# Setup products of a graph attention layer moved into the layer before, norm sums moved to GpSimd, and one group of small products over four PSUM banks

## What is computed

```python
# layer 2, H = 4 heads
Wh = einsum('bni,hoi->bhno', h, W) + bW
e = einsum('bhno,hop->bhnp', Wh, attn)
scores = einsum('bhnp,bhmp->bhnm', e, Wh)
A_mat = tanh(where(adj, scores, 0))
hp = relu(einsum('bhnm,bhmo->bhno', A_mat, Wh))
ha = concat_heads(hp) @ A_w.T;  hf = h @ fc_w.T
coeff = sigmoid(hf @ g1_w.T + ha @ g2_w.T + gbias)
out = hf * coeff + ha * (1 - coeff)
# layer 3, 8 heads of 32, m = embs @ map_w.T + map_b
n = m / maximum(norm(m per head), 1e-8)
cos_adj = (n @ n.T masked) > 0.1
q = m @ q_w.T + q_b;  k = m @ k_w.T + k_b
p_attn = softmax(masked q @ k.T / sqrt(32)) * keep
adj = cos_adj * p_attn
sem = embs @ gcn_map_w.T + gcn_map_b
out = relu((adj @ sem @ gcn_W.T) / (adj.sum(-1) + 1))
```

## Time and profile before

| | before |
|---|---|
| median of 3 runs | 1966.75 us (1961.3 to 1969.16) |
| profiled execution, own time | 1959.6 us |
| its span | 1957.8 us |
| its mean granted TensorE clock | 0.985 |
| busy: TensorE | 1865.9 us (95%) |
| busy: VectorE, ScalarE, GpSimd | 1315.1, 865.8, 613.5 us |

### The profile page before, as it was taken

The page is one execution under the profiler, slowest core; times in us unless marked ns, Lnnn a source line. Parts: engine busy times, 40 slices in busy tenths (PEclk is TensorE's granted clock), DMA queues, the critical chain, the costliest instruction groups (busy, mean ns, idle before and its releaser), DMA issues. The chain is left out here.

```text
span 1957.8 us, 75236 instructions
## 1 busy us (share of the span) xinstructions
PE 1865.9 (95%) x29840; PEld 1739.6 (89%) x29840; DVE 1315.1 (67%) x3055; ACT 865.8 (44%) x1802; POOL 613.5 (31%) x711
## 2 busy tenths in 40 slices
PE   7999999899999789999999999999999799999997
PEld 7889888799999689999999999999999688888886
DVE  6677777567667445555555555555555399999997
ACT  5677777455555322232332332232323245544443
POOL 3565565222222001111111111101111066666665
PEclk9999999899999899999999999999999899999999
DMA  3322222433232211100011110011110022222221
GB/s 111 84 72 76 82 82 77 152 104 95 86 94 87 68 29 35 35 29 27 27 33 33 33 31 24 27 33 33 33 33 28 16 60 67 66 66 66 66 66 61
DMA packets 149394, 113.68 MB, mean 58 GB/s; under 512 B 42945, under 2 KB 148801, under 8 KB 149313
## 3 DMA queue, kind: packets, MB, share of 16 engines
q1 hardware_dynamic: 149312, 112.52, 19.5%
HBM read 78.93 MB, written 33.55 MB: 57 GB/s over the span
## 5 line engine op out<-in xcount | busy, mean ns | idle before, releaser
L272 POOL TENSOR_TENSOR ln_rstd<-ln_var_eps,minus_half 128x2 f32<-128x2 f32 x128 | 91.3, 713 | 695.1 <-DVE ln_var_eps L265 695.1
L1699 ACT ACTIVATE l_cat_hi<-banks 128x512 fp32r<-128x512 f32 x128 | 69.6, 596 | 269.8 <-PE banks L1909 269.8
L179 PE MATMUL banks<-ln_hT_hi,square_w_hi_held 128*128 128x256 f32 x512 | 151.1, 295 | 3.6 <-DVE square_w_lo_held L648 3.2
L289 ACT ACTIVATE ln_h<-ln_x,ln_shift,ln_rstd 128x256 f32<-128x256 f32 x256 | 139.4, 596 | 30.4 <-DVE ln_shift L279 26.6
L179 PE MATMUL banks<-ln_hT_hi,l_g_w_hi 128*128 128x256 f32 x512 | 148.6, 290 | 4.1 <-PEq L2008 4.1
L179 PE MATMUL banks<-l_wh_w_hi,ln_hT_hi 128*128 128x256 f32 (+1 forms) x512 | 148.6, 290 | 0.0
L179 PE MATMUL banks<-l_cat_hi,l_aw_hi 128*128 128x256 f32 x512 | 145.3, 284 | 1.0 <-DVE l_cat_lo L1773 1.0
L180 PE MATMUL banks<-ln_hT_lo,square_w_hi_held 128*128 128x256 f32 x512 | 142.8, 279 | 0.0
L181 PE MATMUL banks<-l_wh_w_hi,ln_hT_lo 128*128 128x256 f32 (+1 forms) x512 | 142.7, 279 | 0.0
L180 PE MATMUL banks<-l_wh_w_lo,ln_hT_hi 128*128 128x256 f32 (+1 forms) x512 | 142.5, 278 | 0.0
L1684 POOL TENSOR_TENSOR l_c_diag<-l_wh,constants_sb 128x256 f32<-128x256 f32 x64 | 38.0, 615 | 333.6 <-DVE l_wh L1766 333.6
(11 more groups left out here) (234 smaller groups left out, 6462.2 us busy)
## 6 DMA issues: line engine op xcount, KB each, us to landing
hidden<-y SPq DMA_DIRECT2D x96, 256.0 KB, 2.1
ln_x<-hidden SPq DMA_DIRECT2D x96, 256.0 KB, 2.7
x_res<-hidden SPq DMA_DIRECT2D x96, 256.0 KB, 2.9
ln_x<-x SPq DMA_DIRECT2D x32, 256.0 KB, 2.8
x_res<-x SPq DMA_DIRECT2D x32, 256.0 KB, 3.0
out<-y SPq DMA_DIRECT2D x32, 256.0 KB, 2.1
...
```

Of the source, the lines that this page charges most:

```text
L179: nc.tensor.matmul(out, lhs(lh), rhs(rh), start=start, stop=False, skip_group_check=True)
L272: self.nc.gpsimd.tensor_tensor(self.rstd[:, g.slot], self.var_eps[:, g.slot], self.core.minus_half[:, 0:PAIRS], ALU.pow).then_inc(self.rst ...
L289: last = self.nc.scalar.activation(self.h[:, u, p, :], self.x[:, u, p, :], ACT.Relu, bias=self.shift[:, u, p:p + 1], scale=self.rstd[:, u, ...
L1699: nc.scalar.activation(in_cat(cat_hi, i), of_two_heads(i), ACT.Relu).then_inc(cat_hi_ready.sem, 1)
```

## The change

Lines are those of the changed kernel where the diff shows them. It does five things.

1. The products attn_wb (`multiply`) and their copies out (`evacuate`) are written into the last two steps of layer 1 on TensorE and ScalarE, in PSUM banks 1 and 2; the placement of b on VectorE into the step before. Their eight chunks are handed out as 1, 1, 2, 2 and 2. `wh_w` gets attnT's memory and is loaded by SP behind layer 1's steps, in two halves; `aw` is loaded in four parts at the setup's start.
2. In the setup the products v are made with one moving column each instead of 257 and no diagonal is needed. wh_w is rounded after G's sixth chunk, aw in four pieces; GpSimd makes half of aw's remainder.
3. The fold of layer 3's weights goes from the setup to the end of layer 2's first step (`first_products`) and uses banks 4 to 7; layer 2's scores of the second step wait for the two small biases (bank 4), its hp products for all six results.
4. Layer 2's hp products become one group of 128 records into banks 5, 6 and 4, 7, with ScalarE's four roundings in a row before the LayerNorm's `apply`.
5. In layer 3 GpSimd sums the squares by five halving additions and clamps them with a sixth operation; VectorE no longer does either. On VectorE `kept` is left out: den = row sum + z, and keep multiplies the reciprocal as before. For the masked rows the factor is zero either way.

```diff
             run_steps(sp, step, groups, 3, ahead=2)
+            if products is not None:
+                products.load_wh_w(sp)
...
+                if products_in(g, 1):
+                    products.evacuate(act, (2, 3))
                 if gn is not None:
                     after(act, v_in_psum, gn.back(2))
                     ln.evacuate_hi(act, gn, B_HT)
                 if b1.exists(groups):
                     evacuate_v()
+                if products_in(g, 1):
+                    products.evacuate(act, (4, 5))
+                if products_in(g, 2):
+                    products.evacuate(act, (6, 7))
...
+                if products_in(g, 1):
+                    after(pe, k_ready, g.back(2))
+                    products.multiply(pe, (0,), early)
                 if not direct and e.exists(groups):
                     transpose_o()
+                if products_in(g, 1):
+                    after(pe, v_act_ready, g.back(2))
+                    after(pe, v_dve_ready, g.back(2))
+                    products.multiply(pe, (1,), early)
+                if products_in(g, 2):
+                    products.multiply(pe, (6, 7), early)
...
+                    after(pool, m_sq_ready, b1)
+                    nc.gpsimd.tensor_tensor(part16[:, u], m_sq[:, u, :, 0:16], m_sq[:, u, :, 16:32],
+                                            ALU.add).then_inc(norm_parts.sem, 1)
+                    after(pool, norm_parts, b1, 1)
+                    nc.gpsimd.tensor_tensor(part8[:, u], part16[:, u, :, 0:8], part16[:, u, :, 8:16],
+                                            ALU.add).then_inc(norm_parts.sem, 1)
+                    after(pool, norm_parts, b1, 2)
+                    nc.gpsimd.tensor_tensor(part4[:, u], part8[:, u, :, 0:4], part8[:, u, :, 4:8],
+                                            ALU.add).then_inc(norm_parts.sem, 1)
+                    after(pool, norm_parts, b1, 3)
+                    nc.gpsimd.tensor_tensor(part2[:, u], part4[:, u, :, 0:2], part4[:, u, :, 2:4],
+                                            ALU.add).then_inc(norm_parts.sem, 1)
+                    after(pool, norm_parts, b1)
+                    nc.gpsimd.tensor_tensor(norm_sq[:, u], part2[:, u, :, 0], part2[:, u, :, 1],
+                                            ALU.add).then_inc(norm_sq_ready.sem, 1)
+                    after(pool, norm_sq_ready, b1, apart=core)
+                    nc.gpsimd.tensor_scalar(norm_cl[:, u], norm_sq[:, u], 1e-16, None, ALU.max).then_inc(norm_cl_ready.sem, 1)
...
-                    nc.vector.tensor_tensor(of_pairs(kept), o[:, :, :, HD].rearrange("q c (p h) -> q c p h", p=PAIRS),
-                                            keep_of_heads, ALU.mult).then_inc(factor_steps.sem, 1)
+                    nc.vector.tensor_tensor(den[:, u], o[:, :, :, HD], z[:, u], ALU.add).then_inc(factor_steps.sem, 1)
                     after(dve, factor_steps, e, 1)
-                    nc.vector.tensor_tensor(den[:, u], kept[:, u], z[:, u], ALU.add).then_inc(factor_steps.sem, 1)
...
-                    nc.vector.reduce_sum(norm_sq[:, u], m_sq[:, u], AX.X).then_inc(norm_sq_ready.sem, 1)
-                    after(dve, norm_sq_ready, b1)
-                    after(dve, r_norm_ready, b1.back(2))
-
-                    nc.vector.scalar_tensor_tensor(out=norm_cl[:, u], in0=norm_sq[:, u], scalar=1e-16, in1=norm_sq[:, u],
-                                                   op0=ALU.max, op1=ALU.max).then_inc(norm_cl_ready.sem, 1)
...
+
+        sp.wait_ge(self.attn_wb_in_psum.sem, 8)
+        for c in range(KC):
+            sp.dma_start(self.wh_w[:, c], rows(self.w["WT"])[:, c]).then_inc(self.wh_w_loaded.sem, 16)
...
+    def multiply(self, pe, chunks, loaded_early):
+
+        nc, ps = self.core.nc, self.core.ps
+        for k in chunks:
+            h, oc = divmod(k, KC)
+            if k == 0:
+                pe.wait_ge(loaded_early.loaded.sem, loaded_early.all)
+                pe.wait_ge(self.b_placed.sem, 1)
+            if k >= 2:
+                pe.wait_ge(self.attn_wb_ready.sem, k - 1)
+            for pc in range(KC):
+                last = nc.tensor.matmul(ps[:, 2 - k % 2, 0:D + 1], self.attnT[:, h * KC + pc, oc * P:(oc + 1) * P],
+                                        self.wb[:, h * KC + pc, :], start=pc == 0, stop=pc == KC - 1)
+            last.then_inc(self.attn_wb_in_psum.sem, 1)
+
+    def evacuate(self, act, chunks):
+        for k in chunks:
+            act.wait_ge(self.attn_wb_in_psum.sem, k + 1)
+            self.core.nc.scalar.activation(self.attn_wb[:, k], self.core.ps[:, 2 - k % 2, 0:D + 1],
+                                           ACT.Copy).then_inc(self.attn_wb_ready.sem, 1)
...
-        B_HP, B_HA = (5, 6), (7, 5)
+        B_HP, B_HA = ((5, 6), (4, 7)), (7, 5)
...
-
-                    if k == 0:
-                        after(pe, cat_lo_ready, c2.back(1), apart=core)
-                        after(pe, blend_steps, c2.back(1), apart=core)
-                    else:
-                        after(pe, cat_lo_ready, c2, 2, apart=core)
+                def product_hp():
+
+
...
+                    if first_products(g.back(1)):
+                        pe.wait_ge(next_weights.made.sem, next_weights.MADE)
+                    after(pe, cat_lo_ready, c2.back(1), apart=core)
+                    after(pe, blend_steps, c2.back(1), apart=core)
                     last = [None, None]
...
+                        if h % 2 == 1:
+                            for b in range(2):
+                                last[b].then_inc(hp_in_psum.sem, 1)
...
+                    if first_products(g.back(1)):
+                        pe.wait_ge(next_weights.made.sem, next_weights.SMALL_MADE)
...
-                if b1.exists(groups):
-                    product_wh(0)
-                    product_wh(1)
-                if c2.exists(groups):
-                    product_hp(1)
-                if b1.exists(groups):
-                    for i in range(2, 6):
+                    product_hp()
+                if b1.exists(groups):
...
+                if first_products(g):
+                    next_weights.fold(pe)
```

The setup block (cut):

```diff
+            for k in range(0, CH, KC):
+                sp.dma_start(aw[:, k:k + KC], rows(weights.w["AwT"])[:, k:k + KC]).then_inc(aw_loaded.sem, 16)
...
+            for k in range(0, CH // 2, KC):
+                pool.wait_ge(aw_split.sem, k // KC + 1)
+                nc.gpsimd.tensor_tensor(aw_lo[:, k:k + KC], aw[:, k:k + KC], aw_hi[:, k:k + KC], ALU.subtract)
...
+            pe.wait_ge(attn_wb_ready.sem, CH)
+            for h in range(H):
+                for jc in range(KC):
+                    k = h * KC + jc
+                    if k >= 6:
+                        pe.wait_ge(g_used.sem, k - 5)
+                    for c in range(KC):
+                        cc = h * KC + c
+                        last = nc.tensor.matmul(ps[:, bank(k), 0:D + 1], wb[:, cc, jc * P:(jc + 1) * P], attn_wb[:, cc, :],
+                                                start=c == 0, stop=c == KC - 1)
+                    last.then_inc(g_in_psum.sem, 1)
+            for h in range(H):
+
+                for jc in range(KC):
+                    k = h * KC + jc
+                    for c in range(KC):
+                        cc = h * KC + c
+                        nc.tensor.matmul(ps[:, B_V, k:k + 1], attn_wb[:, cc, jc * P:(jc + 1) * P], b_col[:, cc:cc + 1],
+                                         start=c == 0, stop=c == KC - 1)
                 for c in range(KC):
                     cc = h * KC + c
-                    left = wb[:, cc, jc * P:(jc + 1) * P] if k < CH else b_col[:, cc:cc + 1].to_broadcast([P, P])
-                    last = nc.tensor.matmul(ps[:, bank(CH + k), 0:D + 1], left, attn_wb[:, cc, :],
...
+            last.then_inc(v_in_psum.sem, 1)
 
         @block.scalar
...
+                round_g(k)
+            act.wait_ge(weights.wh_w_loaded.sem, 16 * KC)
+            nc.scalar.activation(wh_w_hi[:, :, 0:HD], wh_w[:], ACT.Copy).then_inc(wh_w_split.sem, 1)
+            for k in range(6, CH):
+                round_g(k)
+            act.wait_ge(aw_loaded.sem, 16 * CH // KC)
+            for k in range(0, CH, KC):
+                nc.scalar.activation(aw_hi[:, k:k + KC], aw[:, k:k + KC], ACT.Copy).then_inc(aw_split.sem, 1)
 
...
+                rest_of_g(k)
+            dve.wait_ge(wh_w_split.sem, 1)
+            nc.vector.tensor_tensor(wh_w_lo[:, :, 0:HD], wh_w[:], wh_w_hi[:, :, 0:HD], ALU.subtract)
+            dve.wait_ge(v_in_psum.sem, 1)
+            nc.vector.tensor_copy(v_col[:], ps[:, B_V, 0:CH].rearrange("p (h c) -> p h c", h=H))
+            nc.vector.tensor_copy(wh_bias[:, HD:HD + H], ps[:, B_V, CH:CH + H]).then_inc(v_used.sem, 1)
+            dve.wait_ge(aw_split.sem, CH // KC)
+            nc.vector.tensor_tensor(aw_lo[:, CH // 2:], aw[:, CH // 2:], aw_hi[:, CH // 2:], ALU.subtract)
```

224 lines of the change are left out of this document (101 added, 123 removed).

## The result

The changed kernel takes 1915.31 us (median of four runs, 1911.22 to 1920.05) against 1964.03 us of the kernel before in the same comparison: ratio 0.9752, 95% interval 0.9726 to 0.9777. That is 48.7 us less, where 40 were forecast. Of the 11.5 us, 2.7 are the kernel before, whose median is 1964.0 in this comparison and was 1966.75 on record. The profiled execution has a span of 1909.4 us, 48.4 less than before, at a granted clock of 0.988.

What follows compares the result with a forecast made beforehand. TensorE was taken to bound layer 2, VectorE and TensorE to be near their limit in layer 3, with a serial border before layer 2. -12.5 - 14.0 - 13.6 = -40 us from 1966.75 gave 1926.8 us, range 1908 to 1947.

Steps and rivals of the forecast that it cites:

- A: Border of layers 1 and 2: shorter setup, fold moved behind layer 2's first step; -12.5 us, bounds -8 and -17.
- B: Layer 2: one hp group instead of two saves 0.45 us a step in 31 steps; -14.0 us.
- C: Layer 3: GpSimd takes the norm sum, VectorE drops kept, the step falls from 12.04 to 11.5; -13.6 us.
- at full clock, 2.4 GHz, 32 records of this shape take 7.1 us: Setup on TensorE: price of 16 products, two records each; 0.88 us for a chunk of four.
- 48 records, 0.10 us apart: Setup on TensorE: 24 one-column products follow G, from 7.0 to 11.9 us after G's first product.
- the second boundary to wh becomes a plain 0.115: Layer 2 step on TensorE: with one hp group, 2.59 us instead of 3.04.
- the bound of -17: Layer 2, hp grouping: the saving in us if the wait that goes with the second group counts too.
- three engines at 11.0, 11.35 and 11.2 mesh a little worse than one: I take 11.5: Layer 3 step of VectorE, TensorE and GpSimd: -0.54 us in each of 28 steps, -15.1 us.
- 1: GpSimd sets layer 3's pace at 12.0 us, its chain taking 3.75; total 1943 us, chance 0.13.
- rival 4: Layer 3: each small GpSimd add costs 0.71 us, chain 5.0, step 13.2; slower, 1976 us, chance 0.05.
- 2: Layer 2: the hp grouping saves only one boundary of 0.1 us, -3 us; total 1938 us, chance 0.12.
- 3: Layer 3: TensorE's waits carry more than they show, the step follows VectorE to 11.04; 1914 us, chance 0.08.

Runs made afterwards that it cites:

- e2: The changed kernel with kept computed again on VectorE; 1925.25 us, ratio 0.9828.
- e9: The changed kernel with kept computed again on VectorE but written to free columns of a PSUM bank; 1914.60 us, ratio 0.9763.
- e6: The changed kernel with each head's one-column v products placed between that head's two G chunks; 1923.38 us, ratio 0.9817.
- e7: As e6, with aw's rounding on ScalarE and the two large remainders on VectorE moved ahead; 1922.82 us, ratio 0.9799.
- e8: The changed kernel with the 16 attn_wb products back at the setup's start and wh_w loaded there too; 1919.79 us, ratio 0.9800.
- e10: The changed kernel with hp in two groups over four banks, ScalarE and VectorE in the order of the kernel before; 1924.60 us, ratio 0.9812.
- e1: The changed kernel with the sum of squares and the clamp back on VectorE; 1931.35 us, ratio 0.9853.
- e5: The changed kernel with the transposes of n on TensorE made twice in each layer 3 step; 1930.71 us, ratio 0.9848.
- e4: The changed kernel with GpSimd's first addition of the norm sum done twice in each layer 3 step; 1934.10 us, ratio 0.9872.
- e11: The changed kernel with v made as before, 16 records of 257 columns and the diagonal on VectorE; 1914.35 us, ratio 0.9761.
- e12: The changed kernel with layer 3's fold back at the end of the setup; 1917.30 us, ratio 0.9765.

## Why the prediction was right, and where it was not

The time lies in the range, and each part saves time in the way that was forecast. But the sum came out as near as it did because errors cancel in part: A is 2.0 us short, B 0.8 short, C 8.3 over, and 2.9 us of the profiled gain can't be put down to the change.

**A, -10.5 instead of -12.5.** The terms that failed are the lines "at full clock, 2.4 GHz, 32 records of this shape take 7.1 us" and "48 records, 0.10 us apart", as far as they were taken to hold in every execution. At the clock that the profiled execution got, G took 1.7 us and v 3.0 us more. That products there can run at half clock was in the earlier trace rows, nine records at half the pace, and I left it out of the sum. In e2 and e9, at full clock through G and most of v, the block is 15.1 us. The forecast for it is 14.0: 14.9 less the 0.9 of SP's loads, which came (0.97 us) but lie ahead of the block. The 1.1 us between are v, done 12.4 to 13.0 us after G's start and not 11.9, and VectorE's half of aw's remainder, 1.46 and 1.98 us and not 1.14, because GpSimd's half runs into it.

For GpSimd's half I had taken 1.3 us for each subtraction. The second takes 1.26 us, but the first 3.31: it starts 0.09 us behind VectorE's remainder of wh_w (2.28 us, both operands in SBUF) and ends 1.12 us behind its end. In the changed kernel this was hidden; in e6 and e7 it ended the block.

The fold cost about what was said: the first step is 4.3 us longer for 4.9 forecast, and the scores behind it ran at full clock, 2.00 us, which is 1.65 us for 1.7. For the products in layer 1's last steps I took zero, and by layer 1's last addition to y they are worth 1.7; with SP's loads behind it 0.7 of that is left (e8: 0.6).

**B, -13.2 instead of -14.0.** The mechanism is right, a change between kinds of products, and the size of a step is not: 0.37 us and not 0.45. The term that failed is "the second boundary to wh becomes a plain 0.115". The 3.04 us reach twice from the last product ahead of a group to the second one behind it, and where the second group goes two plain intervals take its place, so the sum should have been 3.04 - 2.47 - 0.23 = 0.34 us a step, 10.5 in all. Measured are 0.37 a step, 11.6 in all, and e10 takes the same 11.6 back with four banks kept. The total is nearer than that by luck: 1.6 us come from the step in which nothing lies between the groups, where the second had waited 2.06 us for cat_lo (at 1541.57), a wait that the sum did not have and only the bound of -17 named.

**C, -21.9 instead of -13.6.** The step that failed is "three engines at 11.0, 11.35 and 11.2 mesh a little worse than one: I take 11.5", and 28 steps for 30. They did not mesh worse. (12.04 less 0.67 is 11.37, not 11.35.) Busy time by stretch of 24 steps of the steady part, from the fourth square to the 28th, before and after:

```profile
1597.76:1886.98 289.22, 272.96 (x6339) 248.51 (x6338) 271.09 (x673) 143.68 (x289) 184.27 (x170) 1.00 0.23 67
1572.07:1842.96 270.89, 265.45 (x6339) 248.48 (x6339) 250.72 (x601) 143.62 (x289) 238.23 (x313) 1.00 0.25 72
```

The step goes from 12.05 to 11.29 us, TensorE's busy time in it from 11.37 to 11.06, and its idle time from 0.68 to 0.23. So the step is even shorter than the 11.37 that were to be its floor: the wait for linked carried 0.3 us more than it showed (in e1, where the wait is back, the busy time is 11.37 again), while the wait ahead of attend stayed, which the forecast had taken away. e5 shows TensorE paying every added 0.49 us. The chain's price was right (2.75 us for 3.0), and the first step grew by 0.7 us, not 2. Where TensorE's wait ends last, its busy time is the floor, and I had no row for the allowance on top.

What I costed at 0.20 us was the most fragile part of C. e2 shows kept costing 10 us once GpSimd's additions run beside it: leaving it out, or writing it to PSUM (e9), is what lets the moved sum pay in full. Had the change moved the sum only, its gain in layer 3 would have been 10.2 us and not 20.5 (367.5 less 357.3). e1 shows the other half: the sum is worth 15.4.

**The rivals.** 1 and 4 (GpSimd's chain too long) are excluded by the 2.75 us, but e4 shows how near they were: 0.65 us a step more and nothing is left of C. The point from which rival 4 decides, 4.6 us, was too far: e4's chain of 3.57 already costs layer 3 all of its gain. 2 (only a boundary of 0.1 us) falls with the 2.45 us and e10. 3 gives the nearest time, 1914. Its first half is right, TensorE's waits carried more than they showed; its second, that the step follows VectorE to 11.04, is not: TensorE paces, at 11.26 (e5). The Trainium skill's placing of such a reduction on VectorE (GPSIMD Engine Reference, 4.1 Engine selection), read as advice for this step, would have cost 15.4 us here by e1. Of the other signs named: TensorE waits at the transposes of n only at layer 3's start (1.6 us) and end (0.4), and not at all at the first hp record of step 2.

No kernel tried beats the changed one: e9, e11 and e12 are the same within their intervals.
